# Pair products of embedding rows: one sample per 32-row quarter of TensorE's array, in place of block-diagonal pairs of samples

## The reference

```python
e = jnp.stack([tbl_0[ids[:, 0]], tbl_1[ids[:, 1]], ..., tbl_49[ids[:, 49]]], axis=1)   # (2048, 50, 16)
gram = jnp.einsum('bid,bjd->bij', e, e)
z = gram[:, _I_IDX, _J_IDX]                          # np.triu_indices(50, k=1)
h = jnp.concatenate([z, dense_ctx], axis=1)          # (2048, 1241)
h = jnp.maximum(h @ W_top1 + b_top1, 0.0)            # 512
h = jnp.maximum(h @ W_top2 + b_top2, 0.0)            # 256
y = h @ W_top3                                       # (2048, 1)
```

## Time and profile before

| | |
|---|---|
| median of 3 runs | 813.33 us (812.58 to 814.37) |
| profiled execution, its own time | 811.42 us |
| its span, first to last instruction | 809.6 us |
| mean granted TensorE clock | 0.684 of full (2.4 GHz) |
| PE / PEld / DVE / ACT / POOL busy | 388.4 / 349.9 / 269.2 / 167.8 / 347.4 us |
| pair products (L572, L573) | 2048 matmuls, 177.3 us busy |
| copies to `diag` (L466) | 128, 48.7 us |
| gathers (L353) | 336, 347.0 us |
| evictions (L673) | 64, 52.6 us |

### The profile page before, as it was taken

How to read it: one execution, slowest core, us unless ns; L and a number is a source line. 1 busy time by engine, 2 the same in 40 slices (tenths; PEclk the granted TensorE clock), 3 DMA queues, 4 the chain that set the end, 5 groups by cost and what they waited for, 6 DMA issues and landing times.

```text
span 809.6 us, 15306 instructions
## 1 busy us (share of the span) xinstructions
PE 388.4 (48%) x6544; PEld 349.9 (43%) x6544; DVE 269.2 (33%) x481; ACT 167.8 (21%) x293; POOL 347.4 (43%) x342
## 2 busy tenths in 40 slices
PE   2210017440425547264461836475470847667766
PEld 2100006430414436163461726274370737666766
DVE  5200008980341423424160424135060401433400
ACT  2000005310211225022020314022021214222331
POOL 6777740477372641717264372707355270000000
PEclk9555558665556659578685858577585857888878
DMA  8500002220121213211202122012102020111110
GB/s 294 201 7 7 7 4 86 58 59 7 20 58 27 69 20 91 52 30 23 54 6 65 31 43 58 6 37 71 33 6 40 4 40 5 35 35 36 36 36 2
DMA packets 63122, 36.34 MB, mean 45 GB/s; under 512 B 52160, under 2 KB 58704, under 8 KB 62928
## 3 DMA queue, kind: packets, MB, share of 16 engines
q1 hardware_dynamic: 50580, 32.06, 13.5%
q0 software_dynamic: 10752, 2.77, 4.0%
q10 hardware_dynamic: 1724, 0.52, 0.3%
HBM read 24.26 MB, written 0.13 MB: 30 GB/s over the span
## 4 chain that ended last, share of the span: by engine, by line
issue 30%; PE 25%; another core or an unknown queue 19%; SPq 12%; ACT 5%; DVE 4%; DMA 3%; ACTq 1%; DVEq 0%
SPq L294 12%; PE mlp_ps L582 11%; PE look_ps L551 5%; PE gram_ps L572 3%; PE gram_ps L573 3%; PE mlp_ps L605 2%; ACT gram L673 2%; DVE onehot L378 2%; ACT looked L689 1%; DMA z_both<-gram 1%; ACT z_both L713 1%; ACTq L812 1%; PE gram_ps L551 1%; DVE w_sb L523 1%
## 5 line engine op out<-in xcount | busy, mean ns | idle before, releaser
L353 POOL DMA_INDIRECT emb<-tbl,gidx x336 | 347.0, 1033 | 320.3 <-DVE split L438 218.9
L378 DVE TENSOR_SCALAR onehot<-ids_bc,rows 125x2048 f16<-125x2048 f16 (+1 forms) x144 | 95.9, 697 | 325.6 <-remote 223.5
L551 PE MATMUL look_ps<-parts,onehot 125*128 125x64 f16 x1836 | 96.1, 206 | 216.3 <-issue 140.1
L551 PEld LDWEIGHTS look_ps<-parts,onehot 125*128 125x128 f16 x1836 | 77.3, 106 | 229.5 <-issue 168.5
L582 PE MATMUL mlp_ps<-z_both,w_sb 127*128 127x128 f16 x2112 | 153.1, 238 | 44.9 <-issue 41.0
L582 PEld LDWEIGHTS mlp_ps<-z_both,w_sb 127*128 127x128 f16 x2112 | 140.3, 108 | 45.5 <-issue 41.2
L572 PE MATMUL gram_ps<-turned,diag 128*128 128x50 f16 x1024 | 89.3, 198 | 92.4 <-issue 60.4
L572 PEld LDWEIGHTS gram_ps<-turned,diag 128*128 128x128 f16 x1024 | 74.0, 106 | 93.5 <-issue 92.0
L573 PE MATMUL gram_ps<-turned,diag 128*128 128x50 f16 x1024 | 88.0, 198 | 41.9 <-issue 41.8
L573 PEld LDWEIGHTS gram_ps<-turned,diag 128*128 128x128 f16 x1024 | 72.7, 106 | 59.5 <-issue 59.1
L673 ACT ACTIVATE gram<-gram_ps 114x784 f32<-114x784 f32 x64 | 52.6, 822 | 212.0 <-PE gram_ps L573 151.8
(11 more groups left out here) (30 smaller groups left out, 112.9 us busy)
## 6 DMA issues: line engine op xcount, KB each, us to landing
ids_bc<-ids_dram SPq DMA_DIRECT2D x28, 512.0 KB
emb<-tbl,gidx POOLq DMA_INDIRECT x336
z_both<-gram SPq DMA_DIRECT2D x31, 121.0 KB
z_both<-w SPq DMA_DIRECT2D x1, 2816.0 KB
z_both<-gram SPq DMA_DIRECT2D x31, 90.8 KB
z_both<-gram SPq DMA_DIRECT2D x155, 6.2 KB
z_both<-gram SPq DMA_DIRECT2D x31, 60.5 KB
gram<-small SPq DMA_DIRECT2D x2, 512.0 KB, 4.7
```

The lines of the kernel that those rows point to most:

```text
L353: pool.indirect_dma_start(emb[:, t % TPC, f, :], None, big[f], bass.IndirectOffsetOnAxis(ap=gidx[:, t, f:f + 1], axis=0)).then_inc(gathere ...
L378: nc.vector.tensor_scalar(onehot[0:TP, (SOFF[q] + k) % RING, 0:cnt, :], ids_bc[0:TP, q % IDS_BUFS, 0:cnt, :], rows[0:TP, size, k:k + 1], N ...
L551: last = nc.tensor.matmul(banks[q % len(banks)][:, j % GRP // 2, at:at + width], onehot[0:TP, (SOFF[q] + k) % RING, j % GRP, t * TILE:(t + ...
```

## The change

The block-diagonal buffer `diag`, its memset, its copies on DVE, and the semaphores `diag_ready` and `cleared` go. The stationary operand of a pair product is now a sample's own 64 columns of `turned` in its own quarter of 32 rows (50 of the sample, 14 of the next one, whose products nobody reads). The result goes to partitions 0 to 63 or 64 to 127, by the sample's parity, and to the bank of its quarter. For each sample of a quarter the order is: `turned` for the four quarters, then `turned2` for the four. A tile then has 256 such matmuls for 128, in four runs of 64 (at even g), each of which fills a part of all four banks. `gram_ps` is one buffer of four banks; a run waits until the eviction before is over. PE waits for both transposes at the first run. The order of the samples in a tile is another, undone on the host by the order of `dense` and of the result; ACT's copy of y loses its reordering.

```diff
-HALF = SPQ // 2
-NP = Q // TWO
+SLOTS = SPQ // TWO // EVACS
...
-        turned = sb("turned", [128, 2, TLEN + 80], F16)
-        turned2 = sb("turned2", [128, 2, TLEN + 80], F16)
-        diag = sb("diag", [128, 2, HALF, Q, STEP], F16)
+        turned = sb("turned", [128, 2, TLEN + STEP - NF], F16)
+        turned2 = sb("turned2", [128, 2, TLEN], F16)
...
-        gram_ps = [ctx.enter_context(nc.psum_tensor(f"gram_ps{i}", [128, 2, 512], F32)) for i in range(2)]
+        gram_ps = ctx.enter_context(nc.psum_tensor("gram_ps", [128, Q, 512], F32))
...
-            def set_out(c, t, h):
-
-                if h == 0:
-                    dve.wait_ge(turned_ready, c * (2 * TPC) + (2 * t + 2))
-
-                dve.wait_ge(gram_done, c * (EVACS * TPC) + (EVACS * t + EVACS // 2 * (h - 1) + GRAM_CREDIT))
-                for r in range(Q):
-                    p = slice(32 * r, 32 * r + 32)
-                    last = nc.vector.tensor_copy(
-                        diag[p, h, :, r, 0:NF].bitcast(U32),
-                        turned[p, t % 2, h * HALF * NF:(h + 1) * HALF * NF].bitcast(U32)
-                        .rearrange("p (b j) -> p b j", j=JJ))
-                last.then_inc(diag_ready, 1)
-
...
-                if before or t >= 1:
-                    set_out(c, t - 1, 1)
...
-                set_out(c, t, 0)
...
-            nc.vector.memset(diag[:, :, :, :, :], 0.0).then_inc(cleared, 1)
...
             def dots(c, t, g):
 
-                if g % 4 == 0:
-                    pe.wait_ge(diag_ready, c * (2 * TPC) + (2 * t + g // 4 + 1))
-
-                if g % 2 == 0:
-                    pe.wait_ge(gram_copied, c * (EVACS * TPC) + (EVACS * t + g // 2 + EVAC_CREDIT - 1))
-                for i in range(4):
-                    b = 4 * g + i
-                    for q in range(NP):
-                        at = (NP * i + q) * NF
-                        o = gram_ps[g // 2 % 2][:, g % 2, at:at + NF]
-                        two = diag[:, g // 4, b % HALF, TWO * q:TWO * (q + 1), :].rearrange("p r n -> p (r n)")
-                        nc.tensor.matmul(o, two, turned[:, t % 2, b * NF:(b + 1) * NF], start=True, stop=False)
-                        last = nc.tensor.matmul(o, two, turned2[:, t % 2, b * NF:(b + 1) * NF],
-                                                start=False, stop=True)
                 if g % 2 == 1:
-                    last.then_inc(gram_done, 1)
+                    return
+                e = g // 2
+                if e == 0:
+                    pe.wait_ge(turned_ready, c * (2 * TPC) + (2 * t + 2))
+                pe.wait_ge(gram_copied, c * (EVACS * TPC) + (EVACS * t + e + EVAC_CREDIT))
+                for i in range(SLOTS):
+                    for a in range(TWO):
+                        b = TWO * (SLOTS * e + i) + a
+                        one = slice(b * NF, (b + 1) * NF)
+                        for buf in (turned, turned2):
+                            for r in range(Q):
+                                p = slice(32 * r, 32 * r + 32)
+                                last = nc.tensor.matmul(
+                                    gram_ps[STEP * a:STEP * (a + 1), r, i * NF:(i + 1) * NF],
+                                    turned[p, t % 2, b * NF:b * NF + STEP],
+                                    buf[p, t % 2, one], start=(buf is turned), stop=(buf is turned2))
+                last.then_inc(gram_done, 1)
...
-            pe.wait_ge(cleared, 1)
...
-                src = gram_ps[e % 2][0:rows_used, :, 0:4 * NP * NF]\
-                    .rearrange("p k (b j) -> p j k b", j=NF)[:, 0:NCOL]
+                src = gram_ps[0:rows_used, :, 0:SLOTS * NF].rearrange("p k (b j) -> p j k b", j=NF)[:, 0:NCOL]
...
-                    .rearrange("p j (k b) -> p j k b", k=2)
+                    .rearrange("p j (k b) -> p j k b", k=Q)
```

More of the change, by code:

```diff
@@ L199, in build @@
         ids16 = stage[:, after + 2 * IDS_COLS:after + 2 * IDS_COLS + IDS_COLS // 2].bitcast(F16)
-        gram_ps = [ctx.enter_context(nc.psum_tensor(f"gram_ps{i}", [128, 2, 512], F32)) for i in range(2)]
+        gram_ps = ctx.enter_context(nc.psum_tensor("gram_ps", [128, Q, 512], F32))
         look_ps = ctx.enter_context(nc.psum_tensor("look_ps", [128, 2, 512], F32))
-        start_banks = (look_ps, gram_ps[0])
+        start_banks = (look_ps, gram_ps[:, 0:2, :])
         mlp_ps = [ctx.enter_context(nc.psum_tensor(f"mlp_ps{i}", [128, N1, TILE], F32)) for i in range(2)]
@@ L214, in build @@
         rows_made = sem("rows_made")
-        cleared = sem("cleared")
         hi_made = sem("hi_made")
@@ L230, in build @@
         turned_ready = sem("turned_ready")
-        diag_ready = sem("diag_ready")
         gram_done = sem("gram_done")
@@ L496, in _ @@
             nc.vector.memset(turned[:, :, TLEN:], 0.0)
-            nc.vector.memset(turned2[:, :, TLEN:], 0.0)
             dve.wait_ge(ids_in, 16)
@@ L531, in _ @@
                 slot(NCH - 1, t, True, False)
-            set_out(NCH - 1, TPC - 1, 1)
             split_products(NCH - 1, TPC - 2)
@@ L735, in copy_mlp @@
                     act.wait_ge(y_out[t % 2], c * (16 * TPC // 2) + (16 * (t // 2) + 16))
-                    nc.scalar.activation(y_sb[0:1, t % 2, :].rearrange("p (q a b) -> p a b q", q=NP, a=TWO),
-                                         mlp_ps[1][0:1, 0, :].rearrange("p (a b q) -> p a b q", q=NP, a=TWO),
-                                         ACT.Copy).then_inc(mlp_copied, 1)
+                    nc.scalar.activation(y_sb[0:1, t % 2, :], mlp_ps[1][0:1, 0, :], ACT.Copy).then_inc(mlp_copied, 1)
                     act.wait_ge(mlp_copied, c * (4 * TPC) + (4 * t + 4 + MLPE_CREDIT))
@@ L852 @@
     w1 = np.concatenate([a["W_top1"], np.zeros((1, HID1), np.float32)])[at]
-    dense = a["dense_ctx"].reshape(B // TILE, NP, TWO, SPQ, ND).transpose(4, 0, 2, 3, 1).reshape(DENSE_R, DENSE_K, B)
+    dense = a["dense_ctx"].reshape(NTILES, Q, EVACS, SLOTS, TWO, ND).transpose(5, 0, 4, 2, 1, 3)\
+        .reshape(DENSE_R, DENSE_K, B)
     by_chunk = ids[:, SMALL].reshape(NCH, CHUNK, NS).transpose(0, 2, 1).reshape(NCH * NS, CHUNK)
@@ L877 @@
     r = run_bass_kernel_spmd(nc, [arrays], core_ids=[0])
-    return r.results[0]["y"].reshape(B, 1)
+    by_tile = r.results[0]["y"].reshape(NTILES, TWO, EVACS, Q, SLOTS).transpose(0, 3, 2, 4, 1)
+    return by_tile.reshape(B, 1)
```

## The result

| | before | after |
|---|---|---|
| median of 4 runs each, us | 813.85 (812.58 to 816.54) | 849.32 (844.25 to 852.39) |
| profiled execution, us | 811.42 | 851.05 |
| its span, us | 809.6 | 849.3 |

The ratio is 1.0425, with a 95% interval of 1.0364 to 1.0486: slower, by 35.5 us. The forecast was 872, in a range of 812 to 940.

What follows compares the result with a forecast made beforehand. It took GpSimd's gathers plus TensorE's work in the fast stretches between them to set the period. 811.4 + 26.6 + 16 - 2.4 + 18.4 = 870.0, and 1.9 for the median gave 872 us, range 812 to 940.

Steps and rivals of the forecast that it cites:

- main case: Whole kernel slower, 872 us, or 898 without overlap at half clock; chance 0.50.
- The pair (p): One product matmul with its weight load on TensorE: 25 ns at either clock, bounds 6 and 60 ns.
- full-overlap rival: Product pairs on four quarters run wholly at once, 6.3 ns each, gather stretches do not slip: 802 us, faster; chance 0.13.
- Item 1: Fast stretches between gathers: more product pairs for TensorE, mean 2.2 us in each of 12 periods, +26.6 us.
- Item 2: Gather stretches: 28 more pairs in the mean at 95 ns, half charged, 12 times, +16 us, ends 0 and 32.
- Item 3: VectorE loses 128 copies; gathers beside them shorten by 0.2 us in each of 12 periods, -2.4 us.
- Item 4: Start of the kernel: the memset of the diagonal buffer ends before TensorE starts, so dropping it gives 0.
- Item 5: Last four tiles, without gathers: with one buffer, runs and evictions alternate, 9.24 us for 4.63, +18.4 us in all.
- Half overlap: Quarters overlap by half, 12.5 ns a product pair: 836 us, slower; chance 0.20.
- Exposed weights: Weight loads no longer hidden, 60 ns a product pair: 973 us, slower; chance 0.12.
- slower half clock: No overlap at half clock, 41 ns a product pair there: 898 us; counted within the main case's 0.50.
- first rival: The slower half clock: fast stretches cost 39.7 us and the last four tiles 31.3, 898 us; within the main case's 0.50.

Runs made afterwards that it cites:

- Run 8: The changed kernel with two buffers of two banks and without the second product matmul (2048 products for 4096): 798.80 us against 814.20 before the change, ratio 0.9799.
- Run 7: The changed kernel with its four product banks split into two buffers of two banks, everything computed: 837.32 us against 813.14 before the change, ratio 1.0274.
- run 1: The kernels before and after, both unchanged, run again on chips where the one before takes about 512 us: 512.58 us before, 506.94 after, ratio 0.9879.

## Why the prediction was right, and where its steps failed

The time fell in the range and on the side of the main case, but the sum came out by errors of opposite sign, which is in part luck. On the profiled runs it forecast +58.6, and +39.6 came.

- **The pair (p), the step that failed first.** Taken as 25 ns, between 6 and 60; measured 8.1 and 9.3. The reason I gave, that "a part of the 25 ns is no streaming" and so stays, is refuted: four quarters do overlap, weight loads included. This is close to the full-overlap rival's 6.3 ns, and below the 10 ns at which that rival expected the change to win. The Trainium skill, "TensorE: Matmul & The Clock Gate", Part 3, has matmuls on different row groups run together, starts some 4 ns apart; the trace agrees that they overlap and shows twice that spacing, with a weight load for each. The Trainium skill, "TensorEngine Tiling (Array Packing)", Restrictions and Gotchas, has column tiling lose the fast weight load; the start-to-start time of 8.1 ns, weight load included, shows no cost of it here.
- **Item 1**, fast stretches, +26.6. By its own formula with p = 8.7 ns it is 12 x (0.176 x 8.7 - 2.16) = -7.5. Not measured by itself: the periods around it also hold item 2.
- **Item 2**, gather stretches, +16 with ends 0 and 32: the mis-sized term. What is left of the span's 39.7 when the others are taken out (-7.5 computed from the measured pair, +6.5 measured, and -4.7 for the gathers' 347.0 and 342.3 us) is 45.4 us, beyond the upper end. It is a remainder, and holds the 5.4 us before the seventh tile's gathers too. I priced 28 more pairs a tile at 95 ns and charged half. The traces show that a crawl step is 0.70 or 1.40 us for one instruction, that a stretch passes 118 to 135 matmuls in the mean of each of the four 814-chip traces, and that packs then leave after the stretch and not in it (inside in six of ten stretches before, four after, ten with half the products). That the loss comes by this way is read from the traces, not isolated by a run. Run 8 puts the price of the 2048 extra pairs, inside the stretches and outside, at 38.5 us, 18.8 ns each, twice their time in a quick run.
- **Item 3**, VectorE's copies, -2.4 (0.2 us a tile): -4.7 us of gather time on the 814 chip, -7.7 on the 512 chip. Right in kind, half its size.
- **Item 4**, the memset, 0: nothing came from it.
- **Item 5**, the last four tiles, +18.4. Measured +6.5 (24.45 us for 22.83, four times). The mechanism was right and p was off: with 9.3 ns its own sum is 3 x (0.14 + 0.59 + 0.25 + 0.82) + 0.81 = 6.21 us for 4.63, and four times the difference is 6.3; the evictions of the last four tiles take 6.0 to 6.4 us from first to last. Run 7 takes the wait away, and these tiles fall to 22.5 us.
- **Rivals.** Full overlap, faster (0.13), had the right pair and the wrong second half: it let the gather stretch slip by nothing. It is what happens on a 512 chip, 1.2% faster, since there the stretches pass 500 matmuls. Half overlap's 836 lies nearer to the 849 than the forecast does, by a pair price that wasn't there. Exposed weights and a slower half clock are refuted by the run of 0.81 us at a clock of 0.50.
- **Arithmetic.** Item 1 by its own terms is 26.9 and not 26.6, and the 39.7 and 31.3 of the first rival are 39.2 and 30.7; nothing hangs on it.

Shown, then: on the 814 chips the number of product instructions costs (run 8 against 7) and the single buffer costs (7 against the change). The rest of the change, with the count of products as before and two buffers, is worth 15.4 us there (run 8). 38.5 + 12.0 - 15.4 is 35.1, near the 35.5 of the result, but each term is the difference of neighbouring versions, so the sum closes of itself and is no check. Not shown: why those chips crawl while gathers run, and whether the gathers cause it; it comes with them, outlasts them by 3 us in the stretch shown and by 11 after the fourth tile's, and the kernel with fewer gathers ran on no such chip. One rival the traces speak against: that TensorE waits for its code. Packets of the code queue (q8, "instruction" in the DMA view) took 1.06 us in the mean before and 1.14 after on the 814 chip, 1.07 and 1.08 in run 1. None moved between 664.8 and 698.2, around the whole crawl shown, nor in the kernel before between 21.4 and 125.3, around the one after the fourth tile's gathers. Why some periods stretch to 54 or 57 us is open too; they go with packs that leave after the gathers, but not every such pack makes one.

## What to carry to other kernels

Price an instruction by the stretch in which it is issued: the same pair cost 8 to 9 ns in a quick run, 2.6 ns in the mean where GpSimd covered it, and 18.8 ns in the mean where TensorE was at times let through one instruction at a time. A change that halves each operation and doubles their number can win on one chip and lose on another, so look in the trace for stretches with idle "issue" before splitting work into more instructions. When banks are merged into one buffer, add up run, eviction and hand-over for the tiles that nothing covers; that sum, with the measured pair, came out to 0.2 us in 6.5.

## What the runs showed of the hardware

- The same kernel takes 512 us on some Trainium2 chips and 814 on others, with gathers of the same length (1066 and 1033 ns). On the latter TensorE falls within a gather stretch (7 us into the one shown) to one instruction, matmul or weight load, per 0.70 or 1.40 us, and gets out of it 3 us after the last gather (11 us after the fourth tile's). The cause is open.
- A product of 32 rows, 64 weight columns and 50 moving columns, with its own weight load, four row groups in turn into four banks, starts every 8.1 ns at the full clock (2.4 GHz) and 9.3 at half (1.2), 15% more, where the pairs of 128 rows and 128 columns went from 25 to 41.
- Some VectorE instructions beside gathers lengthen them. In the trace of the kernel before in run 1, gathers with nothing of VectorE beside them took 943 ns in the mean (132 of them), those with transposes alone 943 (30), with the copies to `diag` alone 1068 (22), with compares alone 1162 (50). Without the copies the mean of all fell from 1066 to 1043 ns.
